# Matrix build of a graph network: source one-hots built pair by pair, edge sums issued one place later

## The chip, the cores and the metric

The kernel runs on one core of a Trainium2 chip. The metric is device time in microseconds for one execution. A core has a Tensor engine (PE in the profile; PEld is its weight load), a Vector engine (DVE), a Scalar engine (ACT), a GpSimd engine (POOL) and a Sync engine (SP) that issues DMAs.

## What is computed

Four graph layers on 6250 nodes and 106250 edges, 128 features per node, with a layer norm after each. The first one is a message network with a gated update, the others are graph convolutions with normalised adjacency. Cut to the part that matters here:

```python
def _L0_gnn_ref(x, edge_index, edge_attr, W1, b1, W2, b2, Wih, bih, Whh, bhh):
    src, dst = (edge_index[0], edge_index[1])
    msg_in = jnp.concatenate([x[src], edge_attr], axis=-1)
    h = jax.nn.relu(msg_in @ W1.T + b1)
    messages = h @ W2.T + b2
    agg = jax.ops.segment_sum(messages, dst, num_segments=x.shape[0])
    ...                                   # gated update from agg and x
# L1, L2: degree-normalised sums over edges; L3 (three times): sums weighted by edge_weight
    msg = m[src] * norm[:, None]
    out = jax.ops.segment_sum(msg, dst, num_segments=n_nodes)
```

The edges are sorted by destination. The inputs are fp32.

## The kernel before

Nodes stand in 49 blocks of 128 (NB). The kernel has a set-up, then the stage that this change touches (the matrix build, lines 516 to 991), a short remainder loop for edges that the build could not place, the gated update, and five convolution passes that multiply the node table by matrices written in the build.

The matrix build does two things at once. First, for each destination block u it turns the block's edges into dense matrices: counts per (destination, source) and, from block 16 on (NARROW), weights too. The edges of a block are sorted on chip into slots: one slot per destination row and pair of source blocks, 25 pairs (NK), with a 26th column for self edges. A slot holds the number of the source within its pair (0 to 255), the destination row and three parts of the weight. From the slots the Vector engine makes one-hot matrices, in two halves of 14 and 12 pairs (`one_hots`, line 680): `hot_s` for the source (256 columns per pair, line 688), `hot_d` for the destination (128 columns, line 691) and, from block 16 on, three weighted copies of `hot_d` (`hot_w`, line 699). The Tensor engine multiplies them pair by pair (`blocks`, line 819; lines 840 to 860), the Scalar engine copies the products out of PSUM (lines 930 and 935), and SP stores them. `hot_s` has one buffer for each half, so the comparison of a half waits until the Tensor engine has done the same half of the block before (`filled`).

Second, the edge messages of the first layer run in between, in 208 steps of 4 tiles of 128 edges (HS, TH). GpSimd gathers four tiles of node rows by indirect DMA (line 951) into a ring of 8 steps, and waits for `pre_done` of the step 8 before. The Tensor engine multiplies the edge features (`edge_part`, line 864), the Vector engine builds the one-hots of the step and adds rows and products (`message_sum`, lines 707 and 711), the Scalar engine applies the relu (line 940), the Tensor engine sums two steps by destination (`sum_part`, line 875), and the Vector engine adds that to `acc` (`add_sums`, lines 719 and 720).

The order is written out by hand. The Tensor engine has 541 places: 7 in each of the first 16 blocks, 13 in each of the other 33 (`place`, line 592). The 212 events of the edge messages are spread evenly over them (`at_place`, line 600): at the place of event e the Tensor engine runs `edge_part(e)` and, for even e from 4 on, `sum_part((e - 4) // 2)`. The Vector engine counts the same places by `tick()` (line 722), and does `message_sum(e)` and `add_sums((e - 4) // 2)` 5 ticks (narrow) or 8 ticks (wide) after the place of e. Per block its order is: one-hots of half 0, ranks of the next block's sort (`sort_ranks`, lines 649 to 666), one-hots of half 1, `sort_out` of the next block (lines 672 to 678), and `sort_keys` of the one after (lines 635 to 642). `one_hots` waits for `slots_ready` and `filled`; `sort(u + 1)` on the Tensor engine waits for `lots_ready` of line 658. `message_sum` and `add_sums` wait for `step_sum`, which the last product of a `sum_part` raises: there are four one-hot buffers `hot`, and one PSUM tile `pa` for the sums.

Of the kernel before, what the change touches and what calls it, by code (L numbers as in the profile page):

```python
# [20 lines left out]
P = 128  # L21
# [13 lines left out]
HS = T // TH  # L35
# [9 lines left out]
HALF = 7  # L45
# [95 lines left out]
def build(nc, a, out):  # L141
    with ExitStack() as ctx:
# [99 lines left out]
        with ExitStack() as c:  # L242
# [288 lines left out]

            slots = sb("slots", [P, 2, NV + 1, NK + 1, 2], BF16, c)
            hot_s = sb("hot_s", [P, 2, 2 * HALF, 2 * P], BF16, c)

# [88 lines left out]
            with nc.Block() as block:  # L623
                @block.vector
                def _(dve):
# [43 lines left out]
                    def sort_out(u):  # L669
                        dve.wait_ge(sorted_, u + 1)  # L670
                        found = ps_sort[:, 0:NV * (NK + 1)].rearrange("p (v k) -> p v k", v=NV)
                        V.tensor_copy(slots[:, u % 2, 0:NV], twice(found)).then_inc(slots_ready, 1)
                        V.tensor_copy(self_c[:, u:u + 1], found[:, 0, NK:NK + 1])
                        V.tensor_reduce(self_w[:, u:u + 1], found[:, 2:NV, NK:NK + 1].rearrange("p v k -> p k v"), AX.X,
                                        ALU.add).then_inc(sort_read, 1)
                        dve.wait_ge(slots_ready, 2 * u + 1)
                        V.tensor_scalar(slots[:, u % 2, NV], slots[:, u % 2, 1], 0.0, None,
                                        ALU.is_gt).then_inc(slots_ready, 1)

                    def one_hots(u, h):  # L680
                        m = 2 * u + h
                        n = 2 * HALF if h == 0 else NK + 1 - 2 * HALF
                        ks = slice(2 * HALF * h, 2 * HALF * h + n)
                        if h == 0:
                            dve.wait_ge(slots_ready, 2 * u + 1)
                        if u:
                            dve.wait_ge(filled, fills_of_batch(u - 1, h))
                        V.tensor_tensor(in_pairs(hot_s[:, h, 0:n, :]), in_pairs(per_block(iota_256[:], n)),
                                        per_row_pairs(slots[:, u % 2, 0, ks], 2 * P), ALU.is_equal).then_inc(hots_ready, 1)
                        tick()  # L690
# [103 lines left out]
                def _(pe):  # L794
# [92 lines left out]
                    def first_layer(u, s):  # L887
                        e = at_place.get(place(u, s))
                        if e is not None:
                            if e < HS:  # L890
                                edge_part(e)
                            if e >= 4 and e % 2 == 0:
                                sum_part((e - 4) // 2)

# [1163 lines left out]
```

## Time and profile before

| | before |
|---|---|
| median of 3 runs, us | 4200.97 (4194.1 to 4204.69) |
| profiled execution, us | 4185.11 |
| its span, us | 4183.3 |
| mean granted Tensor clock, share of full | 0.933 |
| PE busy, us (share of span) | 3684.5 (88%) |
| DVE busy | 2600.4 (62%) |
| ACT busy | 1519.8 (36%) |
| POOL busy | 2631.0 (63%) |
| gathers of line 951, us | 1029.0 for 832, 1237 ns each |

A busy share is an average over stages with different limits, so the stage of the change has to be read by itself: its timeline, its stretches and its waits. "L688" is line 688 of the kernel. A wait row names the instruction that waited, what released it, the total in us, how often, and the longest. A gather's time is that of the GpSimd instruction, not of the transfer. The tile names `rows_a` and `x` stand for several buffers that share that room: at lines 691 and 699 `rows_a` holds `hot_d` and `hot_w`, at line 711 `x` holds the ring and the messages.

### The profile page before, as it was taken

The page shows a single profiled execution, that of the slowest core. Times are in us where ns is not written, and L with a number is a line of the kernel's source. Part 1 is how long each engine was busy: PE and PEld are TensorE (multiplying, and loading weights), DVE is VectorE, ACT ScalarE, POOL GpSimd, SP SyncE. Part 2 cuts the span into 40 slices and gives each one's busy share as a digit, 9 for nine tenths or more (in the row PEclk, how much of TensorE's full clock was granted, in tenths as well). Part 3 has the DMA queues.
Part 4 walks back from the last instruction along what each step waited for, and adds up shares of the span by engine and source line. Part 5 has one row for each costly group of instructions (what it writes and reads, how often), then busy time and mean ns, then how long its engine had stood idle before and what let it go on. Part 6 is the DMA issues. An engine that isn't in the chain of part 4 may idle for free. (4 is left out here: it accounts for less than half of the span.)

```text
span 4183.3 us, 80810 instructions
## 1 busy us (share of the span) xinstructions
PE 3684.5 (88%) x30230; PEld 2456.0 (59%) x30230; DVE 2600.4 (62%) x5064; ACT 1519.8 (36%) x3170; POOL 2631.0 (63%) x2363
## 2 busy tenths in 40 slices
PE   5889999999999637888878869999799899989998
PEld 4778888888888523444444435554545555544444
DVE  8888888777777575555533344664366566514665
ACT  3445777776667440000000003332244344303332
POOL 3888788788786016566367747774476566407773
PEclk6778999999999869999989989999899999989999
DMA  4556888888888369999767758998565555529997
GB/s 152 152 147 201 285 284 282 287 278 262 272 269 270 135 202 310 311 317 315 256 217 239 237 162 314 323 328 295 168 216 194 184 194 189 181 87 326 328 323 254
DMA packets 612893, 1019.38 MB, mean 244 GB/s; under 512 B 90889, under 2 KB 417576, under 8 KB 612112
## 3 DMA queue, kind: packets, MB, share of 16 engines
q1 hardware_dynamic: 476700, 773.91, 54.0%
q0 software_dynamic: 90848, 199.74, 16.2%
q10 hardware_dynamic: 44956, 40.55, 3.0%
q8 instruction: 243, 3.98, 0.4%
q14 instruction: 146, 1.19, 0.1%
HBM read 737.12 MB, written 276.78 MB: 242 GB/s over the span
## 5 line engine op out<-in xcount | busy, mean ns | idle before, releaser
L951 POOL DMA_INDIRECT x<-p_table,src_i x832 | 1029.0, 1237 | 310.4 <-issue 242.1
L1541 POOL DMA_INDIRECT rows_b<-x_table,low_src x552 | 575.4, 1042 | 485.4 <-POOLq L159 206.7
L1541 POOL DMA_INDIRECT rows_a<-h_table,low_src x412 | 451.4, 1096 | 231.8 <-issue 121.3
L1620 PE MATMUL po_l3b<-mat_l3b,rows_b 128*128 128x512 f32 (+1 forms) x1372 | 575.7, 567 | 20.2 <-DMA mat_l3b<-weights_fwd 19.2
L930 ACT CAST st_cnt<-ps_mat 128x512 bf16<-128x512 f32 (+1 forms) x825 | 443.1, 596 | 294.4 <-PE ps_deg L845 284.5
L1620 PE MATMUL po_l3a<-mat_l3a,rows_a 128*128 128x512 f32 (+1 forms) x882 | 375.4, 573 | 29.2 <-DMA mat_l3a<-weights_fwd 28.4
L1620 PE MATMUL po_l3c<-mat_l3c,rows_a 128*128 128x512 f32 (+1 forms) x882 | 375.3, 573 | 15.6 <-DMA mat_l3c<-weights_fwd 14.8
L1620 PEld LDWEIGHTS po_l3b<-mat_l3b,rows_b 128*128 128x128 f32 x1372 | 242.9, 196 | 244.6 <-issue 223.4
L1620 PE MATMUL po_l<-mat_l,rows_a 128*128 128x512 bf16 (+1 forms) x1323 | 291.6, 376 | 100.1 <-DVE mat_l L1860 99.3
L860 PE MATMUL ps_mat<-rows_a,hot_s 128*128 128x128 bf16 x4851 | 346.9, 221 | 8.9
L1541 POOL DMA_INDIRECT rows_a<-x_table,low_src x276 | 286.2, 1037 | 93.1 <-issue 84.2
L1775 ACT ACTIVATE t_l<-y_l 128x512 f32<-128x512 f32 (+1 forms) x26 | 15.7, 605 | 886.7 <-DVE y_l L1915 886.7
L1541 POOL DMA_INDIRECT rows_a<-m_table,low_src x276 | 278.2, 1008 | 92.3 <-issue 81.3
L843 PE MATMUL ps_mat<-hot_s,rows_a 128*128 128x256 bf16 x1225 | 317.8, 280 | 0.0
L1620 PE MATMUL po_l<-mat_l,rows_b 128*128 128x512 bf16 (+1 forms) x1323 | 289.6, 373 | 18.9 <-DMA mat_l<-counts_fwd 18.1
L860 PEld LDWEIGHTS ps_mat<-rows_a,hot_s 128*128 128x128 bf16 x4851 | 277.9, 98 | 46.2 <-ACT st_wt L935 36.5
L841 PE MATMUL ps_deg<-slots,hot_s 128*128 128x1 bf16 x2401 | 278.5, 166 | 13.5 <-issue 7.6
L840 PE MATMUL ps_mat<-rows_a,hot_s 128*128 128x128 bf16 x1617 | 248.5, 220 | 26.6 <-DVE rows_a L699 12.2
L1620 PEld LDWEIGHTS po_l<-mat_l,rows_a 128*128 128x128 bf16 x1323 | 123.2, 102 | 240.6 <-DVE mat_l L1860 113.8
L1620 PEld LDWEIGHTS po_l3a<-mat_l3a,rows_a 128*128 128x128 f32 x882 | 158.8, 198 | 174.8 <-issue 145.1
L1728 ACT ACTIVATE split_l3b<-rows_a,low_weight 128x256 bf16<-128x256 f32 x412 | 175.4, 496 | 216.8 <-DMA rows_a<-h_table,low_src 149.4
L1620 PEld LDWEIGHTS po_l3c<-mat_l3c,rows_a 128*128 128x128 f32 x882 | 158.0, 198 | 160.7 <-issue 145.1
(419 smaller groups left out, 7207.2 us busy)
## 6 DMA issues: line engine op xcount, KB each, us to landing
weights_fwd<-st_wt SPq DMA_DIRECT2D x396, 256.0 KB
mat_l<-counts_fwd SPq DMA_DIRECT2D x112, 896.0 KB
mat_l3a<-weights_fwd SPq DMA_DIRECT2D x56, 1792.0 KB
mat_l3c<-weights_fwd SPq DMA_DIRECT2D x56, 1792.0 KB
counts_rev<-st_cnt SPq DMA_DIRECT2D x588, 128.0 KB
rev_l<-counts_rev SPq DMA_DIRECT2D x84, 896.0 KB, 10.8
mat_l3b<-weights_fwd SPq DMA_DIRECT2D x42, 1792.0 KB
counts_fwd<-st_cnt SPq DMA_DIRECT2D x396, 128.0 KB
```

The lines of the kernel that those rows point to most:

```text
L840: nc.tensor.matmul(ps_mat[:, b, q * P:(q + 1) * P], half, rows, start=True, stop=True)
L841: nc.tensor.matmul(ps_deg[:, 2 * k + q:2 * k + q + 1], half, slots[:, u % 2, NV, k, 0:1], start=False, stop=False)
L843: nc.tensor.matmul(ps_mat[:, b, rev_at:rev_at + len(halves) * P], rows, hot_s[:, h, j0 + j, 0:len(halves) * P], start=True, stop=True)
L860: mm = nc.tensor.matmul(ps_mat[:, f % 3, (2 * j + q) * P:(2 * j + q + 1) * P], half, hot_w[:, h, v, j0 + j, :], start=(v == 0), stop=(v == 2))
L930: nc.scalar.copy(st_cnt[:, q, :, j * 2 * P:j * 2 * P + n_col], ps_mat[:, f % 3, :].rearrange("p (d c) -> p d c", d=2)[:, :, 0:n_col]).then ...
L951: pool.indirect_dma_start(ring[:, j % RING, t * FD:(t + 1) * FD], None, p_table, bass.IndirectOffsetOnAxis(src_i[:, j * TH + t:j * TH + t ...
L1541: pool.indirect_dma_start(ring[:, j % RL, t, :], None, table, bass.IndirectOffsetOnAxis(low_src[:, j * TH + t:j * TH + t + 1].bitcast(U32), 0)
L1620: mm = nc.tensor.matmul(po[:, p % 2, k, 0:nb * P].rearrange("p (d c) -> p d c", c=P), rows[:, s, k * P:(k + 1) * P], cols, start=(s == 0 a ...
L1728: part = nc.scalar.activation(split[:, j % 2, 0, t, :], ring[:, j % RL, t, :], ACT.Copy, scale=low_weight[:, j * TH + t:j * TH + t + 1])
L1775: nc.scalar.activation(t1[:, 0:nb, 0:FD], y2[:, f % ys, 0:nb], ACT.Square).then_inc(act_out, 1)
```

## The change

`one_hots` no longer builds the source one-hots of a half by one comparison of two tensors (the column numbers, repeated for each pair, against the slots, repeated for each column). It issues one comparison for each pair, of the 256 column numbers with one fp32 scalar per partition. The scalars stand in a new tile `slot_src`, copied in `sort_out` from the sort's result in PSUM ahead of the copy of all slots. The second half now has 11 pairs and not 12, for `hot_d` and `hot_w` too. The signal `hots_ready` is raised by the last comparison of the half.

`first_layer` on the Tensor engine issues `edge_part(e)` at the place of e as before, and `sum_part` of an event one place later. The Vector engine's ticks, the Scalar engine's and SP's order are as before.

```diff
+            slot_src = sb("slot_src", [P, 2, NK + 1], F32, c)
...
                         found = ps_sort[:, 0:NV * (NK + 1)].rearrange("p (v k) -> p v k", v=NV)
+                        V.tensor_copy(slot_src[:, u % 2], found[:, 0])
                         V.tensor_copy(slots[:, u % 2, 0:NV], twice(found)).then_inc(slots_ready, 1)
...
-                        n = 2 * HALF if h == 0 else NK + 1 - 2 * HALF
+                        n = 2 * HALF if h == 0 else NK - 2 * HALF
...
-                        V.tensor_tensor(in_pairs(hot_s[:, h, 0:n, :]), in_pairs(per_block(iota_256[:], n)),
-                                        per_row_pairs(slots[:, u % 2, 0, ks], 2 * P), ALU.is_equal).then_inc(hots_ready, 1)
+                        for j in range(n):
+                            k = 2 * HALF * h + j
+                            mark = V.tensor_scalar(hot_s[:, h, j, :], iota_256[:], slot_src[:, u % 2, k:k + 1], None, ALU.is_equal)
+                        mark.then_inc(hots_ready, 1)
...
                     def first_layer(u, s):
-                        e = at_place.get(place(u, s))
-                        if e is not None:
-                            if e < HS:
-                                edge_part(e)
-                            if e >= 4 and e % 2 == 0:
-                                sum_part((e - 4) // 2)
+                        at = place(u, s)
+                        if at is None:
+                            return
+                        e = at_place.get(at)
+                        if e is not None and e < HS:
+                            edge_part(e)
+                        e = at_place.get(at - 1)
+                        if e is not None and e >= 4 and e % 2 == 0:
+                            sum_part((e - 4) // 2)
```

## Rows read from the trace of the kernel before

**Rows 1.** the page: busy tenths of VectorE and GpSimd in 40 slices of the span
```profile
DVE  8888888777777575555533344664366566514665
...
POOL 3888788788786016566367747774476566407773
```

**Rows 2.** VectorE timeline, line 688 (start, duration), blocks 0 and 48
```profile
72.14 2.02 DVE L688 TENSOR_TENSOR hot_s<-iota,slots 128x3584 bf16<-128x3584 bf16 x1
...
1336.52 2.08 DVE L688 TENSOR_TENSOR hot_s<-iota,slots 128x3584 bf16<-128x3584 bf16 x1 [2.78 <-PE ps_mat L860]
```

**Rows 3.** stretches: length, busy us (x instructions) per engine, PE clock, DMA share, GB/s
```profile
72.00:360.40 288.40, 249.12 (x2687) 221.37 (x2686) 252.44 (x475) 127.21 (x247) 233.22 (x182) 0.76 0.51 150
387.30:772.50 385.20, 376.05 (x5260) 341.95 (x5258) 319.22 (x565) 278.78 (x562) 308.65 (x252) 1.00 0.88 285
772.50:1336.50 564.00, 539.29 (x7315) 490.51 (x7316) 441.60 (x776) 386.94 (x779) 451.23 (x370) 0.97 0.85 273
```

**Rows 4.** waits in 72:360 (three rows), in 387:772 (two), in 773:1336 (one)
```profile
PE ps_sort L814 <- DVE spread L658: 18.1, 11, 3.9
...
DVE key L635 <- issue: 9.9, 16, 0.9
...
DVE vals L649 <- PE ps_sort L806: 6.1, 4, 3.8
...
DVE hot_s L688 <- PE ps_mat L860: 21.0, 11, 4.1
...
DVE hot L707 <- PE pa L883: 8.4, 8, 2.4
...
DVE x L711 <- DMA x<-p_table,src_i: 52.7, 33, 5.0
```

**Rows 5.** gathers: group of the page; ns min/median/max, first and last start
```profile
L951 POOL DMA_INDIRECT x<-p_table,src_i x832 | 1029.0, 1237 | 310.4 <-issue 242.1
...
L951 POOL DMA_INDIRECT x<-p_table,src_i x832: 940/947/2801, 58.3 to 1339.7; - x167
```

**Rows 6.** timelines of POOL, then of VectorE, over the same 14 us
```profile
309.72 2.63 POOL L951 DMA_INDIRECT x<-p_table,src_i  x1 [0.30 <-issue]
...
319.53 2.15 POOL L951 DMA_INDIRECT x<-p_table,src_i  x1 [0.30 <-issue]
...
309.52 2.02 DVE L688 TENSOR_TENSOR hot_s<-iota,slots 128x3584 bf16<-128x3584 bf16 x1
311.45 1.09 DVE L691 TENSOR_TENSOR rows_a<-iota_up,slots 128x1792 bf16<-128x1792 bf16 x1
...
319.11 1.76 DVE L688 TENSOR_TENSOR hot_s<-iota,slots 128x3072 bf16<-128x3072 bf16 x1
```

**Rows 7.** last gather of step 42 and its message add
```profile
328.91 1.63 POOL L951 DMA_INDIRECT x<-p_table,src_i  x1 [0.30 <-DVE x L711]
...
364.85 0.68 DVE L711 TENSOR_TENSOR x<-pm,x 128x512 f32<-128x512 f32 x1
```

**Rows 8.** one-source instructions: a timeline row, and ns min/median/max of four lines
```profile
1390.07 0.68 DVE L1100 TENSOR_SCALAR hot_s<-iota_row,near 128x128 f32<-128x128 f32 x3
...
L1100 DVE TENSOR_SCALAR hot_s<-iota_row,near x3: 280/280/287, 1390.1 to 1390.5; 128x128 f32<-128x128 f32 x3
...
L1907 DVE TENSOR_SCALAR y_l<-y_l x13: 228/426/439, 1608.6 to 2088.9; 128x512 f32<-128x512 f32 x12, 128x128 f32<-128x128 f32 x1
...
L1909 DVE TENSOR_SCALAR t_l<-y_l,biases x13: 286/486/508, 2149.4 to 2488.0; 128x512 f32<-128x512 f32 x12, 128x128 f32<-128x128 f32 x1
...
L677 DVE TENSOR_SCALAR slots<-slots x49: 164/171/320, 70.0 to 1333.5; 128x52 bf16<-128x52 bf16 x49
```

**Rows 9.** VectorE timeline, a copy of one column from PSUM
```profile
211.57 0.15 DVE L673 COPY self_c<-ps_sort 128x1 f32<-128x1 f32 x1
```

**Rows 10.** a sum on the Tensor engine, and the one-hot build behind it
```profile
486.60 1.90 PE L883 MATMUL pa<-hot,x 128*128 128x64 f32 x16
...
489.85 0.42 DVE L707 TENSOR_TENSOR hot<-iota_row,local 128x256 f32<-128x256 f32 x1
```

## Prediction

> **What bounds the kernel now.** I read the page first: the matrix build fills about the first third of the span, and there the Vector engine and GpSimd are both some eight tenths busy, so busy shares do not name the bound [rows 1]. Next the stretches. The first source comparison of each of the 49 blocks (line 688, the form with 3584 columns) marks its beginning: block 0 at 72.1 us, block 48 at 1336.5 [rows 2], and blocks 16, 17 and 30 at 360.4, 387.3 and 772.5, where I cut the stretches [rows 3]. So a block costs 288.3/16 = 18.0 us in the narrow part (blocks below 16), 385.2/13 = 29.6 us in the first wide part and 564.0/18 = 31.3 us in the last. Busy times and waits of these stretches tell three bounds apart [rows 3, 4].
>
> - Narrow: the Vector engine is busy 252.4 of 288.4 us, with register loads (line 635, 9.9 us) beside, and it waits for the Tensor engine for 6.1 us at its largest such row. The Tensor engine, at a mean granted clock of 0.76, waits 18.1 us for line 658. The Vector engine sets the pace.
> - First wide part: the Tensor engine is busy 376.0 of 385.2 us at full clock, and the Vector engine waits 21.0 us at line 688 for it to free the buffers. The Tensor engine sets the pace.
> - Last part: 564.0 - 539.3 = 25 us without Tensor work, and the Vector engine waits 52.7 us for gathered rows, which it does in neither of the other two.
>
> The third bound is the gather queue. GpSimd runs 832 gathers from 58.3 to some 1340.7 us, 1.54 us apart on the mean. An undisturbed one takes 0.94 us and is followed by a gap of 0.30 us; the mean is 1237 ns, so (1237 - 943) x 832 = 245 us are stalls [rows 5, 6]. The side-by-side timeline shows where they come from. The gather of 309.72 ends at 312.35, 0.81 us after the comparison of line 688 (311.54), and that of 319.53 ends at 321.68, again 0.81 us after a comparison (320.87) [rows 6]. So a gather that begins under a comparison starts its real work when the comparison ends. Sorting all 832 by the Vector instruction that ended 0.81 us before them gives line 688 some 109 us (97 gathers; 37 us narrow, 31 first wide, 41 last), line 699 58 us, lines 655 and 658 56 us. In step 42 the gathers lead the messages by 34 us (330.5 against 364.9) [rows 7]; the ring allows about 8 us more. At 1.54 us for each of the 20.6 gathers of a wide block, 31.7 us, they lose 2 us a block to the Tensor engine, so the lead is gone by the last part, and there the gathers pace everything.
>
> **The comparisons, on the Vector engine.** Now the first comparison of a block takes 1.93 us of the engine (309.52 to the next start, 311.45), for 14 pairs; the second, 1.76 us long with the same overlap of 0.09, 1.67 us for 12 [rows 6]. Together 3.60 us. The new one has 14 + 11 instructions of 256 bf16 columns with a scalar per partition. Nearest row: line 1100, three such instructions on 128 fp32 columns, 280 ns each and 0.68 us for three, so (0.68 - 0.28)/2 = 0.20 us from start to start. Its columns go two a cycle: line 1907 takes 426 ns on 512 columns and 228 on 128, 0.52 ns a column, so 128 columns are 67 ns. 256 bf16 columns cost the same 67 ns if they go four a cycle. The row for that is line 677: 52 bf16 columns in 171 ns, where line 1907's slope and its 162 ns at no columns would give 189 at two a cycle and 175 at four. A scalar per partition costs 60 ns more than a constant (line 1909 against 1907: 486 and 426 ns) [rows 8]. I take 0.20 us. Bounds: 0.14 us, if the fetch of the scalar hid under the instruction before, and 0.27 us at two columns a cycle. The two trains cost 25 x 0.20 = 5.0 us (3.5 to 6.7) against 3.60.
>
> The Trainium skill, "VectorE: DVE Perf Modes", section "The perf-mode tier table (the rule you actually need)", puts tensor_scalar on bf16 at 4x and tensor_tensor at 2x. By columns alone that halves the comparison, to about 1.8 us a block as an estimate; the rows here price the fixed part of 25 instructions and turn the sign.
>
> Added too: the copy of 26 scalars from PSUM, 0.15 us at the length of line 673, 0.06 by start to start with the usual overlap [rows 9]; I take 0.1. Removed: one pair of 12 at line 691 and three times at line 699, 128 columns or 0.07 us each. A gather holds up a short instruction of this kind at times (line 677: longest 320 ns) [rows 8]: 0 to 0.5 us a block, I take 0.2. Sum: 1.4 + 0.1 - 0.1 + 0.2 = +1.6 us in a narrow block, +1.4 in a wide one.
>
> **The same, on GpSimd.** A gather that meets a train waits for the end of one instruction of 0.2 us, not for the rest of 2 us. The trains last 5 us of a block and meet about 3.5 gathers, at 0.1 us each: 17 us in all for 109. More gathers then meet line 691 at its full length: 98 x 1 us, 0.65 gathers begun per us, half of 1 us each is 32 us, 10 of it there already; I take 15 more. The queue becomes about 75 us shorter (bounds 40 and 100). In the last part that is 1.52 - 0.11 + 0.06 = 1.47 us a gather, 30.3 us a block, with 35 to 40 us of lead to draw on. It no longer binds.
>
> **The sums, one place later.** A place is 2.6 us (18.0/7, narrow) or 2.3 us (29.6/13, wide). Nothing on the Tensor engine waits for messages at the sums (no such row among its waits) [rows 4], so the move removes nothing. A sum now stands one place further on in the Tensor queue, behind one more group of matrix products. The Vector engine waits for these sums before it overwrites its one-hots (line 707, 8.4 us in the first wide part) and before it adds them (line 719), and behind that wait stand the next comparison and the next block's sort. For one, the sum of 486.60 ends at 488.50, a place later at some 490.9, and line 707 runs at 489.85 [rows 10]. Over the 104 sums line 707 comes 1 us too early on the mean in the first wide part (2.4 at most but for a few), and in about half of the narrow steps. In the wide part the Vector engine has slack: comparisons are ready 4 to 5 us before they are used. Cost: 0 to 10 us narrow (taken 3, as the Vector engine is later there anyway), 0 to 1.2 us a block wide (taken 0.3, together with the 1.4 us above).
>
> **The sum,** against the profiled execution (span 4183.3, time 4185.1 us; the median of the runs is 4201.0, 16 us higher, carried over). Narrow: 16 x 1.6 = 26, less 4 of waits for the Tensor engine that vanish, plus 3: +25 us. First wide part with block 16: 14 x 0.3 = +4. Last part: 18 x (29.9 - 31.3) = -25. What lies behind, the tail of the build and the layers, stays. Total +4 us: 4189 by the profile, 4205 by the median.
>
> **Rivals.**
> - Cheaper trains (faster): if the scalar's fetch overlaps, a train of 14 costs 2.0 us as line 688 does now; the narrow part grows by 2 instead of 25 us, and the last part returns to 29.6 us a block, -31 us. Total -28: about 4173. For it: the fetch is the only thing that line 1909 has over 1907. Against it: line 1100's 0.20.
> - The Vector engine becomes the bound of the wide part (slower): busy 319.2/13 = 24.6 us a block, register loads 2, new work 1.4 and forced waits of 2 to 3 give 30 to 31. It decides from 29.6 up. At 30.7: 25 + 14 x 1.1 - 18 x 0.6 = +30, 4231. At two columns a cycle it is the same case, harder: 16 x 3.1 = 50 narrow and some 31 a wide block, about 4265.
> - The port is not given up inside a train (slower): gathers then wait for the rest of 2.8 and 2.2 us, stalls grow as the squares, 109 x (7.8 + 4.8)/(4.1 + 3.1) = 191, and the queue ends 80 us later: about 4285. Against it: the gather of 309.72 got in between line 688 and line 691, which follow each other at once [rows 6]. The Trainium skill, "SBUF — State Buffer", section "Who interferes with whom", has tensor_scalar in a two-port mode hold the shared port for reads and writes, tensor_tensor for reads only; no row here shows a train of that kind beside gathers.
> - The change does nothing for the queue (stalls move to the next comparison in line): narrow +25, last part 0, about 4230; counted with the second.
>
> **Numbers.** Forecast, within 12 us of no change: 0.38. Cheaper trains or more relief than I give: 0.25. Vector engine the bound, in either form, or no relief: 0.27. Port held: 0.06. A cooler Tensor clock in the longer narrow part: 0.04. What a measurement here can tell from no change is about 0.3%, 12.6 us. So faster 0.25, same 0.38, slower 0.37. The range leaves out the hardest forms at each end, 4168 to 4248; the forecast's own is 4192 to 4217.
>
> **What would show it.** Source comparisons of about 280 ns, 0.20 us apart (350 and 0.27: two columns a cycle). Mean gather from 1237 down to about 1150 ns. Blocks 19.5 us apart below 16 and 29.9 from 17 to 48, without the step to 31.3. The wait of the message add for gathered rows near nothing. Wrong would be: a narrow part that does not grow (then the Vector engine was not its bound), or gathers as long as before.

## The result and the profile after

The changed kernel takes 4149.65 us, the median of four runs (4145.52 to 4156.0), beside 4201.82 of the kernel before in as many: a ratio of 0.9898 [0.9877, 0.9919]. That is 1.0% faster, or 43 us by the ratio, where the forecast was no change and its range began at 4168. The two medians alone give 52 us, but the kernel before has medians of 4193.1 to 4199.3 us in the later sets of runs, so 4201.82 is at its high end. A second timing of the changed kernel (r1, below) gave 0.9913 [0.9891, 0.9935].

The page of the profiled execution: span, the engines' busy times, VectorE and GpSimd in 40 slices, and the group of the gathers (busy us, mean ns | idle us before them).

```profile
span 4143.7 us, 81967 instructions
...
PE 3666.0 (88%) x30211; PEld 2462.9 (59%) x30230; DVE 2657.9 (64%) x6240; ACT 1528.7 (37%) x3170; POOL 2563.3 (62%) x2363
...
DVE  8898889888888665555523444654456567514665
...
POOL 3766777777775016666267747774476666407773
...
L958 POOL DMA_INDIRECT x<-p_table,src_i x832 | 955.2, 1148 | 356.6 <-issue 243.4
```

The time left the first third, as planned, but not by the amounts planned. Before, the Vector engine stood at 7 tenths in slices 8 to 13 [rows 1]; now it is at 8 or more up to slice 13, since it does more work in less time. The mean gather went from 1237 to 1148 ns [rows 5]. The build ends 26.9 us sooner (1341.9 instead of 1368.8 us); the span is 39.6 us shorter, and the other 12.7 us lie behind the build, in code that is the same.

The stretches between the same blocks (length, then busy us with instructions for PE, PEld, DVE, ACT and POOL, the granted clock, DMA share, GB/s):

```profile
72.50:374.10 301.60, 262.13 (x2684) 234.47 (x2683) 274.45 (x859) 127.77 (x245) 210.11 (x190) 0.72 0.49 144
406.40:780.20 373.80, 368.88 (x5257) 342.93 (x5254) 334.12 (x878) 281.94 (x562) 294.21 (x251) 1.00 0.91 293
780.20:1308.30 528.10, 518.18 (x7287) 481.41 (x7286) 461.18 (x1210) 389.63 (x777) 417.78 (x362) 0.99 0.90 289
```

Against [rows 3]: the narrow part is 301.6 us long for 288.4, so 18.85 us a block for 18.02. The first wide part is 28.75 us a block for 29.63, and the last 29.34 for 31.33. In us, up to the end of the build:

| part | forecast | measured |
|---|---|---|
| blocks 0 to 16 | +25, and 0.3 of block 16 | 333.9 - 315.2 = +18.7 |
| blocks 17 to 29 | +4 | 13 x (28.75 - 29.63) = -11.4 |
| blocks 30 to 47 | -25 | 18 x (29.34 - 31.33) = -35.8 |
| head and tail of the build | 0 | +1.6 |
| sum | +4 | -26.9 |

Of the +18.7 in the first row 5.4 us belong to block 16 alone, which took 32.3 us for 26.9; in r1 it took 28.3, so most of that is chance. The 16 narrow blocks grew by 13.2 us.

Now the new instruction itself: first all of its line (ns min/median/max), then three gathers on GpSimd and the Vector engine over the same time.

```profile
L692 DVE TENSOR_SCALAR hot_s<-iota,slot_src x1225: 266/278/505, 72.5 to 1322.7; 128x256 bf16<-128x256 bf16 x175
...
722.30 0.94 POOL L958 DMA_INDIRECT x<-p_table,src_i  x1 [0.30 <-issue]
723.55 0.94 POOL L958 DMA_INDIRECT x<-p_table,src_i  x1 [0.30 <-issue]
724.79 0.94 POOL L958 DMA_INDIRECT x<-p_table,src_i  x1 [0.30 <-issue]
...
722.76 3.03 DVE L692 TENSOR_SCALAR hot_s<-iota,slot_src 128x256 bf16<-128x256 bf16 x14
725.56 0.41 DVE L711 TENSOR_TENSOR hot<-iota_row,local 128x256 f32<-128x256 f32 x1
```

The 14 comparisons from 722.76 take 2.80 us to the next start (725.56), 0.20 us each; their own length is 278 ns. Three gathers run wholly or in part under them, all at 0.94 us, their undisturbed length. Over the whole build 198 gathers begin between the start and the end of such a train, and are 22.7 us longer together than 943 ns each; before, 103 began under a long comparison and lost 109.4 us. Where more than 0.3 us of the train is left, 175 gathers lose 6.8 us, none more than 0.13. The rest is with 23 gathers that begin in its last 0.3 us: they lose 15.9 us, and nine of them are held for over a microsecond, into the instructions that follow the train at once.

The waits that answer to [rows 4], of the narrow part (two rows), of the first wide part (one) and of the last (one):

```profile
POOL x L958 <- DVE x L715: 38.4, 22, 3.8
...
PE ps_sort L818 <- DVE spread L659: 18.7, 9, 4.5
...
DVE hot_s L692 <- PE ps_mat L864: 0.3, 1, 0.3
...
DVE x L715 <- DMA x<-p_table,src_i: 4.0, 2, 3.1
```

The wait for gathered rows is down from 52.7 to 4.0 us: the queue no longer binds the last part. In the narrow part GpSimd is now ahead and waits itself for a free place in the ring (38.4 us for line 715). And the Vector engine's 21.0 us of slack in the first wide part are down to 0.3 us. It is hardly ahead of the Tensor engine any more, yet the Tensor engine, busy 368.9 of 373.8 us, went faster.

### The profile page after: what moved, and what is told of

Read it like the earlier page. It is cut to its first block and busy times, and to the rows that moved or that the text cites. A ratio compares the mean times of both kernels' runs of the same rounds, so it can differ in the third digit from the quotient of the medians.

```text
span 4143.7 us, 81967 instructions
## 1 busy us (share of the span) xinstructions
PE 3666.0 (88%) x30211; PEld 2462.9 (59%) x30230; DVE 2657.9 (64%) x6240; ACT 1528.7 (37%) x3170; POOL 2563.3 (62%) x2363
## 3 DMA queue, kind: packets, MB, share of 16 engines
q1 hardware_dynamic: 476700, 773.91, 54.6%
q14 instruction: 154, 1.26, 0.1%
## 5 line engine op out<-in xcount | busy, mean ns | idle before, releaser
L958 POOL DMA_INDIRECT x<-p_table,src_i x832 | 955.2, 1148 | 356.6 <-issue 243.4
L1548 POOL DMA_INDIRECT rows_b<-x_table,low_src x552 | 583.8, 1058 | 475.2 <-POOLq L159 203.1
L1627 PE MATMUL po_l<-mat_l,rows_b 128*128 128x512 bf16 (+1 forms) x1323 | 289.9, 373 | 18.7 <-DMA mat_l<-counts_fwd 18.0
L845 PE MATMUL ps_deg<-slots,hot_s 128*128 128x1 bf16 x2401 | 278.8, 166 | 16.3 <-issue 12.9
L692 DVE TENSOR_SCALAR hot_s<-iota,slot_src 128x256 bf16<-128x256 bf16 x1225 | 252.8, 296 | 5.0 <-PE ps_mat L864 3.8
```

What stands on the lines that cost most here:

```text
L692: mark = V.tensor_scalar(hot_s[:, h, j, :], iota_256[:], slot_src[:, u % 2, k:k + 1], None, ALU.is_equal)
L845: nc.tensor.matmul(ps_deg[:, 2 * k + q:2 * k + q + 1], half, slots[:, u % 2, NV, k, 0:1], start=False, stop=False)
L958: pool.indirect_dma_start(ring[:, j % RING, t * FD:(t + 1) * FD], None, p_table, bass.IndirectOffsetOnAxis(src_i[:, j * TH + t:j * TH + t ...
L1548: pool.indirect_dma_start(ring[:, j % RL, t, :], None, table, bass.IndirectOffsetOnAxis(low_src[:, j * TH + t:j * TH + t + 1].bitcast(U32), 0)
L1627: mm = nc.tensor.matmul(po[:, p % 2, k, 0:nb * P].rearrange("p (d c) -> p d c", c=P), rows[:, s, k * P:(k + 1) * P], cols, start=(s == 0 a ...
```

## The experiments

The rest of this document uses four measures of each kernel, taken from the starts of the source comparisons and from the group of the gathers. "To 17" is the time from block 0 to block 17; the next two are us a block in the first wide part and in the last.

| kernel | ratio to before | to 17 | 17 to 29 | 30 to 47 | gather, ns |
|---|---|---|---|---|---|
| before | 1 | 315.2 | 29.63 | 31.33 | 1237 |
| after | 0.9898 [0.9877, 0.9919] | 333.9 | 28.75 | 29.34 | 1148 |
| r1, after again | 0.9913 [0.9891, 0.9935] | 329.0 | 28.69 | 29.35 | 1149 |
| e1, comparisons only | 0.9974 [0.9962, 0.9986] | 330.3 | 29.68 | 29.99 | 1156 |
| e2, sums only | 0.9992 [0.9981, 1.0004] | 308.7 | 30.40 | 31.46 | 1242 |
| e5, edge products late | 0.9912 [0.9898, 0.9926] | 330.0 | 28.41 | 29.70 | 1156 |
| e6, thin relu | 4165.22 us, one run | 334.9 | 29.01 | 29.68 | 1154 |
| e9, before with 3 gathers | 0.9920 [0.9896, 0.9945] | 314.4 | 29.41 | 29.98 | 1235 |
| e10, e2 with 3 gathers | 0.9818 [0.9792, 0.9844] | 309.5 | 28.58 | 28.93 | 1231 |
| e3, two tensors, 1 pair | 1.0016 [1.0000, 1.0032] | 335.6 | 28.99 | 31.77 | 1243 |
| e7, two tensors, 2 pairs | 4141.44 us, one run | 321.9 | 28.76 | 28.91 | 1132 |
| e4, two tensors, 4 pairs | 0.9881 [0.9861, 0.9901] | 312.8 | 28.66 | 29.23 | 1156 |
| e8, two tensors, 7 pairs | 0.9865 [0.9843, 0.9886] | 309.8 | 28.79 | 29.72 | 1183 |
| e11, e8 with the weights cut | 0.9825 [0.9801, 0.9848] | 306.1 | 28.72 | 28.93 | 1152 |

Two profiled executions of one kernel (after and r1) differ by 4.9 us to block 17 and by less than 0.1 us a block behind it, so differences of that size in the third column mean nothing.

**The two parts alone.** e1 is the changed kernel with the old `first_layer`, so that the sums stand where they stood; e2 is the kernel before with the new one.

```diff
 # e2, against before; e1 is the same backwards, against after
                         if e is not None:
                             if e < HS:
                                 edge_part(e)
-                            if e >= 4 and e % 2 == 0:
-                                sum_part((e - 4) // 2)
+                        e = at_place.get(at - 1)
+                        if e is not None and e >= 4 and e % 2 == 0:
+                            sum_part((e - 4) // 2)
```

> The new source comparisons, with the sums at their old place. Theory A (the comparisons shorten the gather queue; the moved sum is what made the wide Tensor pace 28.8 us a block instead of 29.6): narrow blocks 18.9 us as in the changed kernel, wide blocks 29.6 to 29.9 us throughout, without the step to 31.3; about 4175 us. Theory B (the moved sum adds only waits, as the prediction had it): as fast as the changed kernel or faster, 4140 to 4150 us, wide blocks 28.8 or less.

> The old source comparisons, with the sums one place later. Theory A: first wide part near 28.8 us a block, but the gather queue is as long as before (832 gathers, mean near 1237 ns, last one near 1340 us), so the lead is used up sooner and the end of the build hardly moves: within 8 us of the kernel before, about 4200 us. Theory B: 3 to 15 us slower than before, with more wait of the Vector engine at the one-hots of the messages.

> The changed kernel again, timed beside the two below. Ratio to the kernel before 0.988 to 0.992, wide blocks 28.8 to 29.4 us.

e1 alone is 0.26% faster, about 11 us, and e2 makes no difference that can be told. Both together give 0.9 to 1.0%. The comparisons alone do in kind what the sum of the prediction gave them: the narrow part grows (+15.1, for some +22), the first wide part stays, the last returns to 30.0 us a block. What is missing from the forecast is in the step from e1 to after: 29.68 to 28.75 us a block in the first wide part, 29.99 to 29.34 in the last, together 13 x 0.93 + 18 x 0.65 = 24 us. That is the moved sum, which was to remove nothing.

Why then does e2 win nothing? Its waits in the first wide part (two rows) and in the last (one):

```profile
DVE x L711 <- DMA x<-p_table,src_i: 19.1, 13, 4.3
...
DVE hot_s L688 <- PE ps_mat L860: 2.3, 1, 2.3
...
DVE x L711 <- DMA x<-p_table,src_i: 41.0, 28, 3.2
```

Before, the Vector engine waited in the first wide part for the Tensor engine (21.0 us) and not for a gathered row. In e2 it waits 2.3 us for the Tensor engine and 19.1 us for gathers, whose mean length is what it was (1242 ns). Its first wide blocks, 17 to 21, take some 28.3 us each, those behind them, 22 to 29, 31.7 on the mean. The faster Tensor engine uses up the lead of the gathers sooner: the time from the end of a step's last gather to its message add is down to some 5 us at block 24, where it is still 15.5 in the kernel before, which gets there at block 30. From then on every block costs what the queue costs. I had expected 28.8 us throughout that part; only the start of it showed that.

Part of what the queue costs comes by way of the Tensor engine's clock. In the kernel before, the granted clock falls to half (1.2 GHz) three times in the last part, for 10.2 us each. Here are the first of these stretches, one of the same length at full clock (2.4 GHz), and the wait of the Tensor engine just before the first:

```profile
988.70:998.90 10.20, 10.20 (x78) 9.77 (x76) 9.18 (x15) 4.23 (x9) 8.68 (x6) 0.50 0.54 163
1180.00:1190.20 10.20, 9.94 (x140) 8.95 (x139) 9.16 (x14) 6.60 (x14) 8.07 (x8) 1.00 0.92 301
...
987.50 0.23 PE L840 MATMUL ps_mat<-rows_a,hot_s 128*128 128x128 bf16 x1 [3.42 <-DVE rows_a L699]
```

The engine gets through 78 products in place of 140. It had stood still for 3.4 us, waiting for the Vector engine; before the other two it did so for 1.8 and 2.9 us. The time at half clock in blocks 17 to 47, and beside it the waits for gathered rows there: before 30.7 and 52.7 us, e2 78.5 and 60.1 (22.1 of the 78.5 in the first wide part), e3 54.6 and 38.7, e5 30.7 and 12.2, e8 10.2 and 22.1, e4 3.4 and 10.8, e6 10.2 and 7.1, after 10.2 and 4.0, r1 10.2 and 3.8. In e1, e7, e9, e10 and e11 there is neither. So a late row costs its wait and, at times, the slower clock behind it: in the last part of the kernel before at most 15 of the 24 us that separate it from e1. That the waits make the clock fall is argued from this list, not tested by itself.

**The queue by itself.** A direct test is to shorten the queue. e9 is the kernel before with three of the four gathers of each step, e10 is e2 with the same cut; both leave out the rows of every fourth tile, so they serve for timing alone.

```diff
-                        for t in range(TH):
+                        for t in range(TH - 1):
                             pool.indirect_dma_start(
...
-dve.wait_ge(gathered[j % RING], 16 * TH * (j // RING + 1))
+dve.wait_ge(gathered[j % RING], 16 * (TH - 1) * (j // RING + 1))
```

> The kernel before, old comparisons and old sums, but only three of the four gathers of each step are issued, so a quarter of the message rows are left out and the gather queue is a quarter shorter. If the queue paced the last part: 29.7 us a block to the end in place of 31.3, no wait of the message add for gathered rows, and 1.6 x 18 = 29 us less: about 4164 us. If the last part was slower for another reason (the transfers, the stalls of the Tensor clock): 31 us a block stays.

> The same, with three gathers a step, and the sums one place later; the comparisons stay the old ones. If the moved sum helps by itself as soon as the queue is out of the way: 28.9 us a wide block to the end, 27 us less than the run above, and a narrow part 8 us shorter: about 4130 us. If it helps only beside the new comparisons: within 8 us of the run above.

The groups of the gathers, of e9 and of e10 (busy us, mean ns | idle us before them, and what ended most of it):

```profile
L951 POOL DMA_INDIRECT x<-p_table,src_i x624 | 770.6, 1235 | 501.8 <-DVE x L711 288.5
...
L954 POOL DMA_INDIRECT x<-p_table,src_i x624 | 767.9, 1231 | 474.7 <-DVE x L711 260.8
```

One gather is as long as before (1235 and 1231 ns), but there are 624, and GpSimd now waits for the Vector engine to free the ring, 288.5 and 260.8 us: the queue is ahead all the time. e9 takes 4160.5 us, 0.8% less than before. Without the queue, then, the old place of the sum costs 29.41 and 29.98 us a block. e10 differs from it by the place of the sum alone: 28.58 and 28.93 us a block, 4117.07 us, 43 us less. In the profiled executions 33.9 us of that lie in the build. The same edit that is worth nothing in e2 is worth 1% where the queue does not bind.

**What the place of the sum does.** Here is the Scalar engine and, below it, the Tensor engine around the sum of [rows 10] in the kernel before, then the same around a sum in the kernel after (idle time and its releaser in brackets):

```profile
485.88 0.60 ACT L935 COPY st_wt<-ps_mat 128x512 f32<-128x512 f32 x1
488.87 1.07 ACT L930 CAST st_cnt<-ps_mat 128x512 bf16<-128x512 f32 x2 [2.38 <-PE ps_deg L845]
...
485.65 1.11 PE L870 MATMUL pm<-w1eT,rows_a 65*128 65x128 f32 x8
...
488.93 0.83 PE L860 MATMUL ps_mat<-rows_a,hot_s 128*128 128x128 bf16 x12
...
490.57 0.22 PE L840 MATMUL ps_mat<-rows_a,hot_s 128*128 128x128 bf16 x1 [0.24 <-ACT st_wt L935]
...
491.27 0.23 PE L840 MATMUL ps_mat<-rows_a,hot_s 128*128 128x128 bf16 x1 [0.26 <-ACT st_cnt L930]
```

```profile
501.81 1.07 ACT L937 CAST st_cnt<-ps_mat 128x512 bf16<-128x512 f32 x2 [0.65 <-PE ps_deg L849]
...
504.73 0.37 ACT L937 CAST st_cnt<-ps_mat 128x256 bf16<-128x256 f32 x1 [0.83 <-PE ps_deg L849]
...
500.33 1.11 PE L874 MATMUL pm<-w1eT,rows_a 65*128 65x128 f32 x8
...
501.88 0.83 PE L864 MATMUL ps_mat<-rows_a,hot_s 128*128 128x128 bf16 x12
502.54 1.95 PE L887 MATMUL pa<-hot,x 128*128 128x64 f32 x16
```

Before, the edge products (485.65, 1.11 us) and the sum (486.60, 1.90 us) stood back to back, so for 2.7 us, up to 488.33, the Tensor engine filled no buffer that the Scalar engine empties. The Scalar engine had caught up, ran dry for 2.38 us, and then had casts, copies and a relu to do without a pause into the next block, with three buffers `ps_mat` between it and the Tensor engine (in PSUM, the memory that the Tensor engine writes its products to). Two places later, at 490.57 and 491.27, the Tensor engine waits for it to empty one. After the change there is a group of matrix products between the two (501.88): the Scalar engine waits 0.65 and 0.83 us. Its waits for the Tensor engine in the whole first wide part, and those of the weight loads for its copies, of before and then of after (total, times, longest):

```profile
ACT st_cnt L930 <- PE ps_deg L845: 102.2, 74, 3.7
...
PEld ps_mat L860 <- ACT st_wt L935: 13.9, 65, 0.2
...
ACT st_cnt L937 <- PE ps_deg L849: 81.0, 94, 2.2
...
PEld ps_mat L864 <- ACT st_wt L942: 9.6, 45, 0.2
```

The Scalar engine waits more often (94 times for 74) and for shorter times (2.2 us at most for 3.7), 81.0 us in all for 102.2. The Tensor engine's weight loads wait for a free buffer 45 times for 65.

Where the time goes shows when each place of the Tensor engine is measured from its first product of line 845 to that of the next place, over blocks 17 to 29. A block takes 29.83 us before and 28.84 after. The place with edge products and a sum takes 4.19 us on the mean before, the one behind it 1.42; after, 2.46 and 3.20. Together that is no shorter (5.61 and 5.66). What has shrunk is the second place behind the sum: where it has no event, from 1.76 to 1.29 us (18 places; median 1.97 and 1.26), where it has edge products, from 2.66 to 2.40 (15 places). These 33 places make up 12.4 of the 12.9 us between the two. The third place behind is as before, 1.35 and 1.34 us. e1 and e9 have the numbers of before, and r1, e3, e4, e7, e8, e10 and e11 all have those of after, whatever their comparisons and gathers look like.

Two runs test the reading. If it is the lump that counts and not the sum's lateness, it may as well be the edge products that move (e5). If the Scalar engine catching up is what slows the second place behind it, less work for that engine must speed the place up with the lump still there (e6, which leaves the relu out for 504 of the 512 columns, so it too serves for timing alone).

```diff
 # e5, against after
-                        e = at_place.get(at)
+                        e = at_place.get(at - 1)
                         if e is not None and e < HS:
                             edge_part(e)
-                        e = at_place.get(at - 1)
+                        e = at_place.get(at)
                         if e is not None and e >= 4 and e % 2 == 0:
                             sum_part((e - 4) // 2)
 # e6, against e1
-nc.scalar.activation(msg[:, e % 4], msg[:, e % 4], ACT.Relu)
+nc.scalar.activation(msg[:, e % 4, 0:8], msg[:, e % 4, 0:8], ACT.Relu)
```

> The new comparisons; the sums at their old place, and the edge products one place later. So the two pieces of Tensor work that fill no PSUM buffer (1.1 and 1.9 us) stand apart as in the changed kernel, but the sums are not later. Lump theory (while both run back to back, the Scalar engine runs dry, and afterwards the three PSUM buffers make the Tensor engine wait for it): wide blocks 28.9 us as in the changed kernel, a place without an event 1.44 us and not 1.55, time within 10 us of the changed kernel. If it is the later sum that helps (messages not ready in time): 29.7 us a block as with the comparisons alone, about 30 us slower than the changed kernel.

> The new comparisons alone (sums at the old place), and the relu of the messages is applied to 8 of their 512 columns only, so the Scalar engine has 0.4 us less to do in each step. Lump theory: the Scalar engine catches up sooner after the lump, wide blocks at or below 28.9 us. If the Scalar engine is not the limit there: 29.7 us as with the comparisons alone.

e5 leaves the sum at its old place and gives the gain of the changed kernel, 0.9912 for 0.9913; in its Tensor timeline a block takes 28.55 us. Waits of the Scalar engine from 420 to 740 us, of e5 and of e1:

```profile
ACT st_cnt L937 <- PE ps_deg L849: 65.0, 62, 2.8
...
ACT st_cnt L934 <- PE ps_deg L849: 81.2, 62, 3.7
```

As often, and 16 us less in all. e6 keeps the lump (4.19 us at a place with a sum); its second place behind a sum, with no event, takes 1.55 us for 1.77 in e1, and its blocks 29.13 for 29.85. That is the way the theory wants, and less far: I had expected 28.9 or below. So the lump slows the kernel through the Scalar engine and the three buffers; splitting it removes the cost (e5), less Scalar work removes most of it (e6). e5's last part (29.70) is slower than that of after by 0.36 us a block; it has 30.7 us at half clock there, for 10.2, which is worth up to 0.57.

**The length of the trains.** e3, e7, e4 and e8 compare two tensors again, as before, but cut into pieces of 1, 2, 4 and 7 pairs; the sums are late as in after, and the copy to `slot_src` is gone.

```diff
-                        for j in range(n):
-                            k = 2 * HALF * h + j
-                            mark = V.tensor_scalar(hot_s[:, h, j, :], iota_256[:], slot_src[:, u % 2, k:k + 1], None, ALU.is_equal)
+                        for j in range(0, n, m):  # m = 1 (e3), 2 (e7), 4 (e4), 7 (e8)
+                            w, k = min(m, n - j), 2 * HALF * h + j
+                            mark = V.tensor_tensor(in_pairs(hot_s[:, h, j:j + w, :]), in_pairs(per_block(iota_256[:], w)),
+                                                   per_row_pairs(slots[:, u % 2, 0, k:k + w], 2 * P), ALU.is_equal)
                         mark.then_inc(hots_ready, 1)
```

> The changed kernel, but each pair's comparison is one tensor-to-tensor instruction of 256 columns (two a cycle) against the slots, with no copy of scalars. If what counts is that the comparison is cut into short instructions between which a gather can start: trains of about 2.9 and 2.3 us as now (0.21 us each), gathers of 1150 ns, time within 8 us of the changed kernel. If the four columns a cycle or the one tensor operand matter: longer trains or gathers, 15 us or more slower.

> The changed kernel, but the comparison of a half is cut into tensor-to-tensor instructions of four pairs (4, 4, 4, 2 and 4, 4, 3), with no copy of scalars. The cut costs about 0.07 us for each added instruction, so the two trains cost some 3.8 us a block against 5.1: narrow blocks 1.2 us shorter than in the changed kernel, -20 us in all, and a stalled gather waits for 0.6 us at most instead of 0.3, some 15 us more stall, which the lead covers. Theory A: 4125 to 4140 us. If the narrow part is not paced by the Vector engine: no gain over the changed kernel.

> The changed kernel with tensor-to-tensor comparisons of two pairs each, 0.34 us apart. If a gather is shut out only where such instructions are very short (0.21 us apart, a quarter of the gathers that met a train waited for it to end; at four pairs none did): mean stall of a gather that meets a train 0.1 to 0.3 us, wide blocks 28.9 to 29.5 us. If every cut into tensor-to-tensor instructions of less than half a microsecond shuts gathers out: 0.5 us or more, and some 31 us in the last part.

> The changed kernel with each half's comparison in tensor-to-tensor instructions of seven pairs (7 + 7, 7 + 4), 1.0 us long at most. Vector engine 0.2 us a block less than with fours, 1.5 us less than in the changed kernel; gathers that meet one wait 0.4 us on the mean, so the queue is 25 us longer than with fours but 50 shorter than before, about the length that the Tensor engine needs. 4130 to 4145 us; narrow blocks 17.5 to 17.8 us.

Both trains of a block together take 5.3 us in e3, 5.2 in after, 4.4 in e7, 4.0 in e4 and 3.8 in e8 (each from the first start to the last end), and the narrow block 18.98, 18.85, 18.23, 17.83 and 17.52 us, with 17.44 in e2, whose two comparisons take 3.8 us. So a microsecond more in the trains is close to a microsecond more in a narrow block: there the Vector engine does set the pace, as the prediction had it. Pieces of four pairs give nearly all the relief of the queue (1156 ns) with 7 instructions a block in place of 25. e4 takes 4139.26 us and e8 4137.64, for 4149.65 and 4155.08 of the changed kernel. The interval of e4's ratio overlaps with both of the changed kernel's, that of e8 with one, so that they are faster is likely and not certain.

e3 went another way. I had expected it within 8 us of the changed kernel, and it came out at 4198.57 us, the time of before. The group of its gathers, two gathers on GpSimd, the Vector engine over the same time, and the wait for gathered rows in its last part:

```profile
L958 POOL DMA_INDIRECT x<-p_table,src_i x832 | 1033.8, 1243 | 327.7 <-issue 247.5
...
410.03 3.05 POOL L958 DMA_INDIRECT x<-p_table,src_i  x1 [0.30 <-issue]
413.38 3.30 POOL L958 DMA_INDIRECT x<-p_table,src_i  x1 [0.30 <-issue]
...
408.02 2.91 DVE L691 TENSOR_TENSOR hot_s<-iota,slots 128x256 bf16<-128x256 bf16 x14
410.85 1.08 DVE L695 TENSOR_TENSOR rows_a<-iota_up,slots 128x1792 bf16<-128x1792 bf16 x1
411.85 0.41 DVE L711 TENSOR_TENSOR hot<-iota_row,local 128x256 f32<-128x256 f32 x1
412.19 0.68 DVE L715 TENSOR_TENSOR x<-pm,x 128x512 f32<-128x512 f32 x1
412.79 3.08 DVE L703 TENSOR_TENSOR rows_a<-rows_a,slots 128x1792 bf16<-128x1792 bf16 x3
...
DVE x L715 <- DMA x<-p_table,src_i: 37.3, 27, 4.7
```

The trains are nearly as short as those of after, 2.83 us for this one of 14 (408.02 to 410.85; 2.93 on the mean), so 0.20 us from start to start, yet the gathers are as long as in the kernel before. That of 410.03 begins late in the train and ends at 413.08, 0.81 us after line 711 has ended (412.26): it was let in neither between two comparisons nor at the starts of 410.85 and 411.85. That of 413.38 ends at 416.68, 0.81 us after the three of line 703 have (415.87). Of the 190 gathers that begin under a train 47 are held up for over a microsecond, 100.0 us in all, where after has 198, nine and 22.7. The difference is in those that begin with more than 0.3 us of the train left: 173 lose 82.5 us, up to 3.3 us one, for 175 and 6.8 in after. The queue binds again, 37.3 us of waits in the last part. e7, whose pieces are 0.34 us apart, does not show it:

```profile
L958 POOL DMA_INDIRECT x<-p_table,src_i x832 | 942.1, 1132 | 344.1 <-issue 232.3
```

157 of its gathers begin under a train and lose 15.6 us, none more than 0.3 us. Why a train of two-tensor comparisons 0.20 us apart shuts gathers out, and one of comparisons with a scalar as far apart does not, the runs do not tell; that it is so, e3 beside after shows.

**Both kernels beaten.** The long two-tensor instructions that are left are the weighted copies at line 699, to which 58 us of stalls were put down before. e11 is e8 with these cut in sevens as well.

```diff
                         for v in range(3):
-                            V.tensor_tensor(in_pairs(hot_w[:, h, v, 0:n, :]), in_pairs(hot_d[:, h, 0:n, :]),
-                                            per_row_pairs(slots[:, u % 2, 2 + v, ks], P), ALU.mult).then_inc(hots_ready, 1)
+                            for j in range(0, n, 7):
+                                w, k = min(7, n - j), 2 * HALF * h + j
+                                mark = V.tensor_tensor(in_pairs(hot_w[:, h, v, j:j + w, :]), in_pairs(hot_d[:, h, j:j + w, :]),
+                                                       per_row_pairs(slots[:, u % 2, 2 + v, k:k + w], P), ALU.mult)
+                            mark.then_inc(hots_ready, 1)
                             tick()
```

> The kernel with comparisons in sevens, and from block 16 on each of the three weighted copies of a half also in two instructions (7 + 7, 7 + 4). Costs the Vector engine 0.4 us of each wide block, where it has slack, and nothing in the narrow part. Gathers held by these copies wait 25 us less in all. With sevens alone the queue was again just the limit in the last part (29.7 us a block against the Tensor engine's 28.9, and 22 us of waits for gathered rows). If the queue theory holds: 28.9 to 29.2 us a block there and 10 to 15 us less in all, 4122 to 4130 us. If the Vector engine is at its limit in the wide part: 29.3 us or more in the first wide part too, and no gain.

The span of its profiled execution, and the gathers:

```profile
span 4132.5 us, 81087 instructions
...
L961 POOL DMA_INDIRECT x<-p_table,src_i x832 | 958.5, 1152 | 310.9 <-issue 237.9
```

Its median is 4123.41 us, 0.9825 [0.9801, 0.9848], 76 us less than before in the same set of runs and the fastest of the kernels that gather everything; its interval still touches that of e8. The gathers are at 1152 ns for 1183 in e8, no row of waits for gathered rows is left in the last part, and that part takes 28.93 us a block, the Tensor engine's pace of e10.

## Why the prediction was wrong

- **The trains: right.** From the first start to the start of the next instruction they take 2.77 and 2.21 us, 5.0 us a block, where I took 0.20 us for each of 25. The row bears out the faster of my two readings: 278 ns for 256 bf16 columns, as line 1100 has for 128 fp32 ones, where two a cycle would have been 350. The copy into `slot_src` takes 0.175 us.
- **The narrow part: right in kind, twice too high.** +0.8 us a block (18.02 to 18.85) for +1.6. That is not the sums' doing: with them in the old place it is +0.9 (e1, 18.93). Between e2 and after, both with late sums, it is +1.4, close to my term. So in the kernel before the Vector engine's path had some half a microsecond a block that was not work, which longer trains fill and late sums remove too (e2 17.44, e10 17.62 for 17.99 in e9). My sum took off 0.25 for it. The part of it that I could name, the wait for the sort [rows 4], fell from 6.1 to 3.0 us (line 650); the rest is not located.
- **The relief of GpSimd: right in size, in part by luck.** 89 ns less in each of 832 gathers, 74 us for my 75. Sorted as in the prediction, by the Vector instruction that ended 0.81 us before the gather, the comparisons went from 109 to 6.7 us, better than my 17. In return the one-hot build of the messages, line 711 (707 before), went from 5.5 to 32.8 us, a term that my sum did not have, and line 695 from 10.4 to 17.1, where I had added 15. The port is given up between two comparisons of the new form, so that rival is out. The Trainium skill, "SBUF — State Buffer", section "Who interferes with whom", has tensor_scalar in a two-port mode take the pair of ports shared with GpSimd for the whole instruction, and tensor_tensor with both inputs in SBUF contend with GpSimd's reads alone. For short instructions in a row the runs show the two-tensor form as the one that holds gathers (e3, 82.5 us for 173, against after, 6.8 us for 175).
- **"The move removes nothing": the step that failed.** I looked for something that waits for the messages at the sums, found no row, and costed the move as pure lateness, 3 us and 0.3 a block. What it removed stood in another row, that of the Scalar engine waiting for the Tensor engine in lumps of up to 3.7 us, 102.2 us in the first wide part. I had read the Tensor engine's 376.0 busy of 385.2 us as "the Tensor engine sets the pace", and a wait of the Scalar engine as idle time that costs nothing. It cost 1.0 us a block: 29.83 to 28.84 in the Tensor timeline, and 43 us between e9 and e10. Its 98% busy left room for 3%. In the waits they stand as many short ones, 0.2 us at line 860, which I had passed over; those rows fell by 6 us for the weight loads and by 3 for the products. Most of the rest was inside the busy time itself: for the same products it fell from 376.05 to 368.88 us. The ends of the products are modelled, so a pace set by another engine can read as busy; the length of the places, above, shows it.
- **The last part: right in mechanism, too small.** I had 29.9 us a block and e1 shows 29.99; the 0.65 below that is the moved sum again, 12 us of the -35.8. That the queue took part of its price by way of the half clock, 30.7 us of it before and 10.2 after, I had overlooked, though the 0.97 stood in my rows.
- **The Vector engine as the bound of the wide part** did not come, but the cover for it is gone. In e1 the Vector engine still waits for the Tensor engine to free `hot_s`, in blocks 17 to 48:

```profile
DVE hot_s L692 <- PE ps_mat L864: 41.9, 24, 5.8
```

In after that is 0.3 us in the first wide part and 0.9 in the last. The faster Tensor engine took nearly all of it: with the old, short comparisons and no queue the wait is 46.2 us in blocks with the old place of the sum (e9, 380 to 1300 us) and 6.3 with the new one (e10). The kernels with shorter trains gain mainly elsewhere, in the narrow part: 312.8 us to block 17 in e4, 309.8 in e8 and 306.1 in e11, for 333.9 and 329.0. The prediction's two ways to a faster kernel, cheaper trains or more relief of the queue, are not what happened either.

**What stays open.** The build accounts for 26.9 us of the gain in the profiled executions (32.4 in r1), the ratios for 43 and 36. The stage behind the build took between 2801.8 (after) and 2826.1 us (e11) in kernels with the same code there, 2814.5 in before; a dozen microseconds of the gain lie in that scatter and are not located. The parts of e1 and e2 add up to -14 us, and to -36 to -43 as one change: the interplay by way of the queue is shown by e9 and e10, its size in each block of e2 is not.

## What to carry to other kernels

An engine that reads as 98% busy can still be paced by the one that empties its buffers: look whether work that fills no buffer stands in one lump (here 2.7 us with three buffers), and put a group of buffer-filling work between the pieces before adding buffers or cutting work. Where two limits lie within a few per cent, a change that lifts one may measure as nothing until the other is lifted as well, so each is to be timed with the other out of the way. And if long two-input instructions on the Vector engine hold up indirect gathers, cutting them into a few pieces buys nearly all of the relief: here three or four pieces of up to 1024 columns, where one instruction for each pair costs 1.2 us a block more.

## What the runs showed of the hardware

- Gathers that begin under a run of comparisons with a scalar for each partition, 278 ns long and 0.20 us apart, with more than 0.3 us of it left, take 0.94 us as if alone: 6.8 us lost by 175. Under a run of two-tensor comparisons 0.20 us apart 173 such gathers lose 82.5 us; 0.34 us apart, 120 lose 14.8 us.
- A gather that is shut out can stay so over the starts of several instructions that follow at once: that of 410.03 in e3 took 3.05 us, over those of lines 695 and 711. In after it happens only to gathers that begin in the last 0.3 us of a train, nine times for over a microsecond. In the kernel before, one got in between lines 688 and 691 [rows 6].
- A second two-tensor comparison of 256 bf16 columns starts 0.20 us behind the first, of 512 columns 0.34 us and of 1024 columns 0.60 us (e3, e7, e4).
- In these kernels the granted Tensor clock fell to half in the wide blocks only where gathered rows came late, for 3.4 to 78.5 us in all, and in none of the five kernels without such waits. At half clock the engine did 78 products in 10.2 us, for 140.
